# Softmax attention: 49-row stacks per head, two heads at a time in two 64-row tiles, four stack buffers, maxima in pairs

## Chip, core and metric

The kernel runs on one core of a Trainium2 chip. The metric is the device time of one execution in microseconds (us). Engines: PE is TensorE, PEld its weight loads, DVE VectorE, ACT ScalarE, POOL GpSimd, SP the engine that issues the DMAs. A name with q behind it (PEq) is that engine's sequencer.

## What is computed

The reference is a chain of two layers on x of shape (8, 1024, 256): softmax attention and routed experts, then linear attention and a gated mixture of experts. The change touches only the softmax attention:

```python
qkv = x @ w_attn
q, k, v = jnp.split(qkv, 3, axis=-1)          # 16 heads of 16 features, t = 1024
attn = jnp.einsum('bhqd,bhkd->bhqk', q, k) * scale
attn = jnp.where(causal[None, None], attn, -jnp.inf)
sm = jax.nn.softmax(attn, axis=-1)
out = jnp.einsum('bhqk,bhkd->bhqd', sm, v)
```

## The kernel before

`build` calls nine phases, one after the other, with all engines meeting between them. `phase_softmax_attention` (lines 288 to 643) works on 32 groups (8 batches times 4 groups of 4 heads, `GH`). For each head it stacks high and low halves of q and k along the partitions: q as high, high, low, low and k as high, low, high, low, 16 rows each, so that one product over the stack is the sum of the four part products. Row 64 (`SR`) of the q stack holds minus the row maximum and row 64 of the k stack holds ones; the rest up to 128 is zero. Three such buffers (`NBUF`) are filled in turn by 10 DMAs each (`load`, lines 403 to 410), the last of which puts zeros into the row of the maxima.

Each group goes through two score passes:

* The maxima pass, one group or more ahead. 39 pieces (`pieces`, `piece`, lines 545 to 559), each up to 512 columns wide in one of three PSUM buffers (`m_ps`, `MBUF`). A piece is one matmul for each of its heads and, where it lies on the diagonal, one bf16 matmul of an identity with a causal mask behind them. DVE reduces each piece to its maximum (line 493) and gives the buffer back (`m_free`). At the end the maxima are turned by PE (line 563), negated by ACT (line 505) and put into row 64 by a DMA (`row`, line 412).
* The score pass. 24 steps (`steps`): two halves h of the queries, key blocks k, and pairs p of heads. A step is two matmuls (line 578) into one of two buffers of `e_ps`, and one exponential on ACT (line 523) into `pr`. Two steps make a unit, 12 units a group. On the diagonal POOL masks the exponentials (line 475). Two units later (`LAG = 2`) `products` (line 582) multiplies them with v in four column tiles of 32, in plain float32, which the trace shows as 8 matmuls for each unit. The sums `o_ps` are copied by ACT (line 511) twice a group, and PE may start the next sums only when SP has seen that copy (`o_free`).

PE's order is written out by hand in `group` (line 598): step by step the wait for the exponential two steps back, the scores, the pieces that `share` gives to this step, and after each second step the products of an earlier unit. From step 19 (`MEND`) the pieces belong to the group after the next, and PE waits there for that group's stacks (`stack_loaded`, line 608). SP issues those loads in the same group, right after the first output (lines 423 to 426). PE executes in order: whatever stands behind a wait waits too.

## Time and profile before

| what | value |
|---|---|
| median of 3 runs | 4138.56 us (4131.36 to 4143.86) |
| span of the profiled execution | 4136.6 us, mean granted clock 0.892 |
| PE busy in the span | 3388.8 us (82%) |
| DVE, ACT, POOL busy in the span | 2384.2, 1507.4, 839.8 us |
| first and last score matmul of this phase | 303.9 and 1411.0 us |
| first and last matmul of the maxima pass | 265.4 and 1383.4 us |

The profiled execution has no other time than its span; the median of the runs is 2 us above it. Busy shares are averages over phases with different limits; the softmax attention is a little over a quarter of the span, and only its own rows say what bounds it. The start of a PE instruction is recorded and its end is modelled, so consecutive matmuls overlap in the rows by their latency.

### The profile page before, as it was taken

The numbers are of one execution on the slowest core, as the hardware profiler recorded it, in microseconds if no ns is written. First come the engines' busy times: TensorE is split into PE (matmuls) and PEld (weight loads), VectorE is DVE, ScalarE is ACT, GpSimd is POOL, SyncE is SP. The second block draws the span as 40 slices with busy tenths as digits, with TensorE's granted clock in tenths as the row PEclk, the third lists the DMA queues.
The fourth block names the chain that finished last, engine by engine and source line by source line (L and its number), as shares of the span: only waits on it lengthen the run. The fifth ranks groups of instructions, "written<-read, shape, count | busy, mean of one in ns | idle before, by whom it ended". The sixth has DMA issues, their size and how long they took to land. (4 is left out here: it accounts for less than half of the span.)

```text
span 4136.6 us, 62031 instructions
## 1 busy us (share of the span) xinstructions
PE 3388.8 (82%) x21377; PEld 2546.4 (62%) x21377; DVE 2384.2 (58%) x5007; ACT 1507.4 (36%) x2286; POOL 839.8 (20%) x1006
## 2 busy tenths in 40 slices
PE   6859999999999766579564776999566599999998
PEld 5735555555555465569343564777466488888887
DVE  5546666666666377683123785555477644444544
ACT  2315555555555433334002662000133323333333
POOL 0021111111111122234674663000122100000000
PEclk9879999999999878789656998999777699999999
DMA  6884666666666256563565996666344433233331
GB/s 191 234 146 60 85 85 85 85 81 84 84 85 84 74 184 200 183 214 127 132 139 138 345 346 217 210 207 206 108 153 153 158 84 85 86 81 81 81 81 51
DMA packets 452026, 570.37 MB, mean 138 GB/s; under 512 B 94544, under 2 KB 300400, under 8 KB 450672
## 3 DMA queue, kind: packets, MB, share of 16 engines
q1 hardware_dynamic: 440064, 544.45, 52.3%
q0 software_dynamic: 10240, 14.16, 2.0%
q10 hardware_dynamic: 1648, 10.81, 0.7%
q8 instruction: 42, 0.69, 0.1%
q14 instruction: 32, 0.26, 0.0%
HBM read 329.62 MB, written 238.61 MB: 137 GB/s over the span
## 5 line engine op out<-in xcount | busy, mean ns | idle before, releaser
L493 DVE TENSOR_REDUCE att_mx<-att_m_ps 128x1 f32<-128x512 f32 (+4 forms) x1248 | 743.5, 645 | 381.6 <-PE att_m_ps L554 324.1
L523 ACT ACTIVATE att_pr<-att_e_ps 128x1024 f32<-128x1024 f32 (+3 forms) x768 | 597.7, 811 | 366.5 <-PE att_e_ps L578 362.3
L551 PE MATMUL att_m_ps<-att_ks,att_qs 128*128 128x512 f32 (+3 forms) x1536 | 470.3, 377 | 99.5 <-PEq L39 95.4
L578 PE MATMUL att_e_ps<-att_qs,att_ks 128*128 128x512 f32 (+3 forms) x1536 | 466.9, 386 | 10.5 <-PEq L39 9.0
L475 POOL TENSOR_SCALAR_AFFINE_SELECT att_pr<-att_pr 128x256 f32<-128x256 f32 x512 | 206.7, 407 | 938.5 <-PEq L571 931.9
L578 PEld LDWEIGHTS att_e_ps<-att_qs,att_ks 128*128 128x128 f32 x1536 | 249.1, 194 | 239.9 <-issue 186.7
L551 PEld LDWEIGHTS att_m_ps<-att_ks,att_qs 128*128 128x128 f32 x1536 | 280.0, 195 | 155.2 <-issue 93.7
L594 PE MATMUL att_o_ps<-att_pr,att_vs 128*17 128x512 f32 (+3 forms) x3072 | 330.1, 502 | 0.0
L2116 DVE TENSOR_TENSOR ffn_hid<-ffn_gate,ffn_u_ps 128x512 f32<-128x512 f32 x192 | 132.1, 688 | 249.5 <-PE ffn_u_ps L698 213.1
L2164 ACT ACTIVATE ffn_hh<-ffn_hid 128x512 fp32r<-128x512 f32 x192 | 121.4, 633 | 421.5 <-DVE ffn_hid L2120 319.3
L698 PE MATMUL ffn_y_ps<-ffn_wld,ffn_hh 128*128 128x256 f32 x768 | 216.9, 282 | 0.0
L698 PE MATMUL ffn_y_ps<-ffn_whd,ffn_hh 128*128 128x256 f32 x768 | 216.2, 281 | 0.0
L2126 DVE TENSOR_TENSOR ffn_hl<-ffn_hid,ffn_hh 128x512 fp32r<-128x512 f32 x192 | 133.0, 693 | 141.7 <-ACT ffn_hh L2164 141.7
L698 PE MATMUL ffn_y_ps<-ffn_whd,ffn_hl 128*128 128x256 f32 x768 | 214.2, 279 | 0.0
L1059 PE MATMUL prj_t_ps<-prj_ident,prj_xn 128*128 128x128 f32 x256 | 62.7, 422 | 161.8 <-DVE prj_al L984 159.1
L554 PE MATMUL att_m_ps<-att_causal,att_identb 128*128 128x128 bf16 (+2 forms) x736 | 188.9, 257 | 0.0
L2086 POOL TENSOR_TENSOR ffn_rs<-ffn_ve,ffn_mhalf 128x4 f32<-128x4 f32 x16 | 16.1, 1007 | 824.7 <-POOLq L39 824.7
L698 PE MATMUL ffn_g_ps<-ffn_xh,ffn_whg 128*128 128x512 f32 x384 | 153.5, 400 | 28.0 <-DMA ffn_xl<-x_low 20.6
L1940 ACT ACTIVATE lin_ot<-lin_o_ps 128x1024 f32<-128x1024 f32 x32 | 32.9, 1027 | 367.1 <-PE lin_o_ps L1970 357.7
L2162 ACT ACTIVATE ffn_gate<-ffn_g_ps 128x512 f32<-128x512 f32 x192 | 114.5, 596 | 134.8 <-PE ffn_g_ps L698 134.8
L1059 PEld LDWEIGHTS prj_t_ps<-prj_ident,prj_xn 128*128 128x128 f32 x256 | 48.7, 219 | 172.3 <-DVE prj_al L984 168.0
L698 PE MATMUL ffn_g_ps<-ffn_xh,ffn_wlg 128*128 128x512 f32 x384 | 152.8, 398 | 0.0
(286 smaller groups left out, 8168.2 us busy)
## 6 DMA issues: line engine op xcount, KB each, us to landing
prj_o<-attended SPq DMA_DIRECT2D x32, 1024.0 KB, 5.0
ffn_wt<-weights SPq DMA_DIRECT2D x16, 2048.0 KB, 16.0
att_qs<-q_high SPq DMA_DIRECT2D x64, 256.0 KB, 5.8
att_qs<-q_low SPq DMA_DIRECT2D x64, 256.0 KB, 8.7
att_ks<-k_high SPq DMA_DIRECT2D x64, 256.0 KB, 12.3
att_ks<-k_low SPq DMA_DIRECT2D x64, 256.0 KB, 15.9
attended<-att_ot SPq DMA_DIRECT2D x64, 256.0 KB, 2.2
prj_x<-x SPq DMA_DIRECT2D x32, 512.0 KB, 5.9
```

Source lines behind the costliest of these rows:

```text
L475: e.affine_select(out=blk, in_=blk, compare_op=ALU.is_ge, fill=0.0, base=0, pattern=[[0, 2], [1, P]], channel_multiplier=-1).then_inc(mask ...
L493: e.reduce_max(mx[:, h, heads[0]:heads[-1] + 1, q], src, AX.X).then_inc(m_free, 1)
L523: e.activation(pr[:, u % NPR, 2 * p:2 * p + 2, 0:w], e_ps[:, s % 2, :, 0:w], ACT.Exp).then_inc(exp_done, 1)
L551: ins = e.matmul(out[:, i], qs[:, j, hd, q * P:(q + 1) * P], ks[:, j, hd, h * BLK:h * BLK + w], start=i == 0, stop=h != q // 4, skip_group ...
L554: ins = e.matmul(out[:, :, w - P:w], identb[:], causal[:].unsqueeze(1).broadcast_to((P, len(heads), P)), start=False, stop=True, skip_grou ...
L578: i = e.matmul(e_ps[:, s % 2, n, 0:w], ks[:, j, hd, k * P:(k + 1) * P], qs[:, j, hd, (h + 1) * BLK - w:(h + 1) * BLK], start=True, stop=True)
L594: i = e.matmul(o_ps[32 * hd:32 * hd + VW, BLK - w:BLK], vs[:, j, k, hd * VW:(hd + 1) * VW], pr[:, u % NPR, hd, 0:w], start=k == 0, stop=k ...
L698: i = e.matmul(out, a, b, start=first and n == 0, stop=last and n == len(terms) - 1, **kw)
L2116: product_ = e.tensor_tensor(hid[:, c % 2], gate[:, c % 2], u_ps[:, c % 2], ALU.mult)
L2126: e.tensor_tensor(hl[:, c % 3], hid[:, c % 2], hh[:, c % 3].bitcast(fp32), ALU.subtract).then_inc(hl_ready, 1)
L2162: e.activation(gate[:, c % 2], g_ps[:, c % 2], ACT.Silu).then_inc(gate_ready, 1)
L2164: e.activation(hh[:, c % 3], hid[:, c % 2], ACT.Copy).then_inc(hh_ready, 1)
```

## The change

The fourth part product (low times low) is dropped, so a stack has 48 rows and the row of the maxima is row 48. Two heads share one buffer: heads 0 and 1 of the group at partitions 0 to 48, heads 2 and 3 at 64 to 112. Each matmul of both passes then covers 48 or 49 rows from partition 0 or 64, and matmuls for the upper and the lower half follow each other in pairs, into different PSUM banks. The ones of the k stack are now written once, beside and beyond the stack's rows, so no DMA of zeros is needed, and the maxima product leaves their row out. There are four stack buffers, loaded by 12 smaller DMAs and one for v, three groups ahead. The row of the maxima is written by two DMAs.

The pieces come in pairs, one of each half: 21 pairs, 42 pieces. The masks of a diagonal pair come first (two bf16 matmuls over all 128 rows), then the score matmuls add to them. Units with at most 256 columns take one step with both head pairs, so there are 20 steps in 12 units. `products` stands at the head of a unit and takes the unit three back (`LAG = 3`), the same place in PE's order as before. The copy of the sums, though, is now made after the exponential of the third unit (`of_unit[LAG - 1]`) and of the seventh. PE turns to the group after the next at unit 8 (`TURN`) and takes the maxima at step 16 (`MAXIMA`), the first of unit 9.

```diff
-    NBUF = 3
+    NBUF = 4
     NPR = 4
     MBUF = 3
-    SR = 4 * HD
+    LAG = 3
+    HALF, MAXROW = P // 2, 3 * HD
-        qs = ph.sb("qs", [P, NBUF, GH, T], f32r)
-        ks = ph.sb("ks", [P, NBUF, GH, T], f32r)
+        qs = ph.sb("qs", [P, NBUF, 2, T], f32r)
+        ks = ph.sb("ks", [P, NBUF, 2, T], f32r)
...
-        steps = [(h, k, p) for h in range(2) for k in range(4 * h + 4) for p in range(2)]
+        units = [(h, k) for h in range(2) for k in range(4 * h + 4)]
+        steps = []
+        for u, (h, k) in enumerate(units):
+            steps += [(u, (0, 1))] if width(h, k) <= BLK // 2 else [(u, (0,)), (u, (1,))]
...
+                both = 2 * keys(q, h) <= BLK and q != 1
+                (partial if h == q // 4 else whole).extend((q, h, ps) for ps in (((0, 1),) if both else ((0,), (1,))))
+        pairs, taken = [], 0
+        for n, piece in enumerate(partial):
+            pairs.append(piece)
+            while taken < len(whole) and taken + 1 <= len(whole) * (n + 1) / len(partial):
+                pairs.append(whole[taken])
+                taken += 1
...
+        TURN, MAXIMA = 8, 16
...
                 def load(g, j):
-                    for name, dst, parts in (("qh", qs, (0, 1)), ("ql", qs, (2, 3)),
-                                             ("kh", ks, (0, 2)), ("kl", ks, (1, 3))):
-                        for r in parts:
-                            e.dma_start(dst[r * HD:(r + 1) * HD, j].bitcast(fp32), src_rows[name][g]
-                                        ).then_inc(stack_loaded[j], 16)
+                    for n in range(2):
+                        for dst, parts in ((qs, ("qh", "qh", "ql")), (ks, ("kh", "kl", "kh"))):
+                            for r, name in enumerate(parts):
+                                at = n * HALF + r * HD
+                                e.dma_start(dst[at:at + HD, j].bitcast(fp32), src_rows[name][g][:, 2 * n:2 * n + 2]
+                                            ).then_inc(stack_loaded[j], 16)
                     e.dma_start(vs[:, j], v_rows[g]).then_inc(stack_loaded[j], 16)
-                    e.dma_start(maxima_row(j), zero[:]).then_inc(stack_loaded[j], 16)
...
                     if loads:
-                        load(g + 2, (nxt + 1) % NBUF)
+                        load(g + 3, (nxt + 2) % NBUF)
...
-                        if s == 2 * LAG - 1 and not first:
+                        if s == of_unit[LAG - 1][0] and not first:
                             outputs(1, NPR)
-                        if s == 2 * (LAG + 3) + 1:
+                        if s == of_unit[LAG + 3][0]:
                             outputs(0, NPR + 4)
...
+                def maxima_pair(j, i):
+                    q, h, ps = pairs[i]
+                    w, masks = keys(q, h), h == q // 4
+                    out = [m_ps[:, (2 * i + n) % MBUF, 0:len(ps) * w].rearrange("p (n w) -> p n w", w=w)
+                           for n in range(2)]
+                    for n in range(2):
+                        if masks:
+                            e.wait_ge(m_free, 2 * i + n + 1)
+                            e.matmul(out[n][:, :, w - P:w], identb[:],
+                                     causal[:].unsqueeze(1).broadcast_to((P, len(ps), P)), start=True, stop=False,
+                                     skip_group_check=True)
+                    for m, p in enumerate(ps):
+                        for n in range(2):
+                            if not masks and m == 0:
+                                e.wait_ge(m_free, 2 * i + n + 1)
+                            rows = slice(n * HALF, n * HALF + MAXROW)
+                            ins = e.matmul(out[n][:, m], qs[rows, j, p, q * P:(q + 1) * P],
+                                           ks[rows, j, p, h * BLK:h * BLK + w], start=not masks and m == 0,
+                                           stop=m == len(ps) - 1, skip_group_check=True)
...
                 def scores(j, s):
+                    u, ps = steps[s]
+                    h, k = units[u]
                     w = width(h, k)
+                    for m, p in enumerate(ps):
+                        for n in range(2):
+                            rows = slice(n * HALF, n * HALF + MAXROW + 1)
+                            i = e.matmul(e_ps[:, s % 2, n, m * w:(m + 1) * w], ks[rows, j, p, k * P:(k + 1) * P],
+                                         qs[rows, j, p, (h + 1) * BLK - w:(h + 1) * BLK], start=m == 0,
+                                         stop=m == len(ps) - 1, skip_group_check=True)
...
+                    for u in range(UNITS):
+                        if not (first and u < LAG):
+                            products(j, u - LAG)
+                        if u == TURN and more2:
+                            e.wait_ge(stack_loaded[nxt2], LOADS)
+                            take(e, (stack_loaded[nxt2], LOADS))
+                        due = list(share[u]) if (more2 if u >= TURN else more) else []
+                        for s in of_unit[u]:
+                            for i in due[:1]:
+                                maxima_pair(nxt2 if u >= TURN else nxt, i)
+                            due = due[1:]
+                            exponentials(s, first)
+                            if s == MAXIMA and more:
+                                maxima()
+                            scores(j, s)
+                        for i in due:
+                            maxima_pair(nxt2 if u >= TURN else nxt, i)
```

## Rows read from the trace of the kernel before

**Rows 1.** Busy time in stretches of the stage, first and last of three: length, engines, clock.
```profile
core 0: us, PE busy (x) PEld busy (x) DVE busy (x) ACT busy (x) POOL busy (x), PEclk, DMA share, GB/s
304.00:650.00 346.00, 325.98 (x2093) 178.29 (x2093) 230.85 (x393) 194.34 (x264) 62.27 (x154) 0.98 0.58 77
...
1000.00:1411.00 411.00, 388.28 (x2544) 209.23 (x2545) 258.79 (x442) 237.42 (x327) 78.81 (x196) 0.99 0.54 75
```

**Rows 2.** Timeline of PE alone, two groups: start, length, instruction, idle before and its releaser.
```profile
827.39 0.63 PE L551 MATMUL att_m_ps<-att_ks,att_qs 128*128 128x128 f32 x4 [2.42 <-PEq L39]
...
862.50 0.64 PE L551 MATMUL att_m_ps<-att_ks,att_qs 128*128 128x128 f32 x4 [2.43 <-PEq L39]
```

**Rows 3.** Who waited for whom, 304 to 1411 us: total us, times, longest.
```profile
PE att_m_ps L551 <- PEq L39: 58.0, 29, 2.7
...
PEld att_e_ps L578 <- ACT att_pr L523: 43.9, 70, 0.9
...
PEld att_m_ps L551 <- DVE att_mx L493: 26.4, 68, 1.9
```

**Rows 4.** DMA issues, 304 to 1411 us: count, size, median us to landing.
```profile
att_qs<-att_zero SPq DMA_DIRECT2D x29, 16.0 KB, 17.0
```

**Rows 5.** Timeline of all engines, 803 to 822 us.
```profile
803.53 0.41 PE L594 MATMUL att_o_ps<-att_pr,att_vs 128*17 128x128 f32 x8
...
804.01 0.60 ACT L511 ACTIVATE att_ot<-att_o_ps 128x512 f32<-128x512 f32 x1
...
804.68 0.39 PE L551 MATMUL att_m_ps<-att_ks,att_qs 128*128 128x512 f32 x1
...
805.00 1.05 PE L594 MATMUL att_o_ps<-att_pr,att_vs 128*17 128x512 f32 x8
...
807.48 0.84 PE L594 MATMUL att_o_ps<-att_pr,att_vs 128*17 128x384 f32 x8
...
808.25 0.73 PE L578 MATMUL att_e_ps<-att_qs,att_ks 128*128 128x512 f32 x2
...
808.82 0.63 PE L551 MATMUL att_m_ps<-att_ks,att_qs 128*128 128x512 f32 x2
...
809.08 1.94 ACT L523 ACTIVATE att_pr<-att_e_ps 128x1024 f32<-128x1024 f32 x2 [1.39 <-PE att_e_ps L578]
...
809.29 0.62 PE L578 MATMUL att_e_ps<-att_qs,att_ks 128*128 128x512 f32 x2
...
809.92 3.28 SPq L410 DMA_DIRECT2D att_qs<-att_zero  x1
...
822.31 1.05 PE L594 MATMUL att_o_ps<-att_pr,att_vs 128*17 128x512 f32 x8
```

**Rows 6.** Timeline of the weight loads (PEld): one alone, two together, then eight of products.
```profile
276.18 0.19 PEld L551 LDWEIGHTS att_m_ps<-att_ks,att_qs 128*128 128x128 f32 x1 [0.41 <-DVE att_mx L493]
...
277.97 0.30 PEld L551 LDWEIGHTS att_m_ps<-att_ks,att_qs 128*128 128x128 f32 x2 [0.41 <-DVE att_mx L493]
...
819.30 0.13 PEld L594 LDWEIGHTS att_o_ps<-att_pr,att_vs 128*17 128x17 f32 x8 [0.31 <-issue]
```

**Rows 7.** Groups by line and shape, 304 to 1411 us: busy, mean ns, idle before.
```profile
L493 DVE TENSOR_REDUCE att_mx<-att_m_ps 128x1 f32<-128x512 f32 x744 | 475.3, 685 | 103.3 <-PE att_m_ps L551 54.4 <-PE att_m_ps L554 47.9
L523 ACT ACTIVATE att_pr<-att_e_ps 128x1024 f32<-128x1024 f32 x384 | 379.3, 1027 | 225.0 <-PE att_e_ps L578 224.4
```

**Rows 8.** Timeline of the start: the first group's reduces, a DMA issue, the first scores.
```profile
269.29 20.10 DVE L493 TENSOR_REDUCE att_mx<-att_m_ps 128x1 f32<-128x384 f32 x35 [0.25 <-PE att_m_ps L554]
...
278.97 11.89 SPq L410 DMA_DIRECT2D att_qs<-att_zero  x1
...
303.93 1.19 PE L578 MATMUL att_e_ps<-att_qs,att_ks 128*128 128x512 f32 x2 [9.00 <-PEq L39]
```

**Rows 9.** Busy time in two stretches of the start, columns as in rows 1.
```profile
275.00:280.00 5.00, 4.55 (x17) 2.48 (x17) 5.00 (x9) 0.00 (x0) 0.00 (x0) 1.00 1.03 121
...
283.00:287.00 4.00, 4.00 (x12) 2.20 (x11) 4.00 (x9) 0.00 (x0) 0.00 (x0) 0.57 1.19 170
```

More of the change, by code:

```diff
@@ L363, in keys @@
             return min(BLK, (q + 1) * P - h * BLK)
+        units = [(h, k) for h in range(2) for k in range(4 * h + 4)]
+        UNITS = len(units)
+        steps = []
+        for u, (h, k) in enumerate(units):
+            steps += [(u, (0, 1))] if width(h, k) <= BLK // 2 else [(u, (0,)), (u, (1,))]
+        NS = len(steps)
+        of_unit = [[s for s in range(NS) if steps[s][0] == u] for u in range(UNITS)]
         def diagonal(s):
-            h, k, p = steps[s]
+            h, k = units[steps[s][0]]
@@ L367, in diagonal, with masks_before @@
             return k * P >= h * BLK
+        NDIAG = sum(diagonal(s) for s in range(NS))
+        def masks_before(u):
+            return sum(diagonal(s) for v in range(-LAG, u + 1) for s in of_unit[v % UNITS])
+        whole, partial = [], []
+        for q in range(KB):
+            for h in range(q // 4 + 1):
+                both = 2 * keys(q, h) <= BLK and q != 1
+                (partial if h == q // 4 else whole).extend((q, h, ps) for ps in (((0, 1),) if both else ((0,), (1,))))
+        pairs, taken = [], 0
@@ L369, in shares @@
+        for n, piece in enumerate(partial):
[3 more added lines that the diff above has]
+                taken += 1
+        NPAIR, NPC = len(pairs), 2 * len(pairs)
+        TURN, MAXIMA = 8, 16
+        assert NPC % MBUF == 0 and taken == len(whole) and width(*units[steps[MAXIMA][0]]) <= BLK - P
+        assert MAXIMA % 2 == 0 and steps[MAXIMA][0] > TURN
         def shares():
-            order = list(range(MEND, len(steps))) + list(range(MEND))
@@ L372, in shares @@
-            load = [keys(q, h) * len(heads) + 96 for q, h, heads in pieces]
-            work = [width(*steps[s][:2]) + 160 for s in order]
+            order = list(range(TURN, UNITS)) + list(range(TURN))
+            load = [keys(q, h) * len(ps) + 64 for q, h, ps in pairs]
+            work = [sum(width(*units[u]) * 2 * len(steps[s][1]) + 80 for s in of_unit[u]) for u in order]
             out, n, done, due = {}, 0, 0.0, 0.0
-            for s, w in zip(order, work):
+            for u, w in zip(order, work):
@@ L376, in shares @@
                 due += w * sum(load) / sum(work)
-                out[s] = []
-                while n < NPC and done + load[n] / 2 <= due:
+                out[u] = []
+                while n < NPAIR and done + load[n] / 2 <= due:
                     done += load[n]
-                    out[s].append(n)
+                    out[u].append(n)
                     n += 1
+            assert n == NPAIR
             return out
         share = shares()
-        NDIAG = sum(diagonal(s) for s in range(len(steps)))
@@ L386, in phase_softmax_attention @@
-        UNITS = len(steps) // 2
-        LAG = 2
-        def masks_before(u):
-            return sum(diagonal(2 * (v % UNITS)) for v in range(-LAG, u + 1)) * 2
         src_rows = {n: d.rearrange("(g h d) t -> g d h t", h=GH, d=HD)
```

154 lines of the change are left out of this document (58 added, 96 removed).

## The prediction

> **What bounds the stage now.** I read the slices of the span for where this phase lies, then busy time in stretches, the timeline of one group, the waits, the issues of SP, and the groups by shape. PE is busy 94% of the stage, DVE 63 to 67%, ACT 56 to 58%, at a granted clock of 0.98 or 0.99, so the 2.4 GHz level nearly throughout [rows 1]. The same piece comes again 862.50 - 827.39 = 35.1 us later [rows 2]: that is one group, and 31 such periods make up the stage. PE bounds it, but its busy time hides drains and its own order. Inside each period it stands still once, 2.42 us, at the sequencer's wait for the stacks of the group after the next [rows 2]; in all 58.0 us in 29 waits [rows 3]. SP issued the last DMA of that load at 809.92 and such a DMA lands 17.0 us later [rows 4, 5], hence at 827, which is when PE goes on.
>
> **One group before, in PE's time.** A score pass has 4608 columns for each head (the unit widths 512, 384, 256, 128, four times 512, and again 512 to 128), 18432 for four. At 2.4 GHz 512 columns take 0.213 us, a pass 7.7, two passes 15.4. Eight product matmuls take 1.05 us for 512 columns and 0.41 for 128 [rows 5], that is four times the clock for each column, with the four heads side by side: 4608 columns give 7.7 us. Masks: 32 blocks of 128 columns, 1.7. A weight load of 128 columns costs 0.11 where it isn't hidden, two of them taking 0.30 and one 0.19 [rows 6]; so a 128-column block costs 0.11 instead of 0.053, which adds 1.7 for scores, pieces and masks. Going over to the products and back: two scores behind products take 0.73 instead of 0.62 and start 0.07 before the products' modelled end (808.25 against 807.48 + 0.84), where they otherwise start 0.16 to 0.17 before it (809.29 against 808.82 + 0.63) [rows 5]: 0.21 on the way out. Products start 0.07 before the end of the piece ahead (805.00 against 804.68 + 0.39) [rows 5]: 0.10 on the way in. 12 units, 3.7. Turning the maxima 0.3. Sum 30.5. Waits: 2.4 for the stack, and 43.9 and 26.4 us over 31 periods for exponentials and reduces [rows 3], 2.3. Total 35.2 against 35.1.
>
> **What the change takes away.**
> * The stack wait. Loads are issued a whole period earlier, and there is no DMA of zeros behind them: -2.4 a group. Issuing costs SP 13 DMAs instead of 10, some 0.4 us each more, hidden because the next output isn't ready for several units. The two rows of the maxima are issued at unit 9, units 10 and 11 hide their landing.
> * The streams. If two row tiles run at the same time, both passes go from 15.4 to 7.7 us. No row of this trace shows two row tiles. Bounds: nothing gained (0), all (7.7). The nearest row are the four column tiles of the products, which share the array fully, and whose eight weight loads take 0.13 us together [rows 5, 6]. I take the whole 7.7, with the loads of a pair side by side too.
>
> **What it adds.**
> * Mask excursions. Masks cover 128 rows, the matmuls around them 64, so 13 of the 21 pairs now leave the row tiles and come back. Price from both sides: 0, if full and half height mix freely, or that of the products' excursion with a load of 128 columns exposed on the way in, 0.10 + 0.11 = 0.21 and 0.21 back. Seven of the 13 stand directly behind products, where one of the two is paid anyway: 7 x 0.21 + 6 x 0.42 = 4.0 us. Narrow pairs cost their load (0.4 a pass, 8 blocks of 128 as 4 pairs: 4 x 0.054 = 0.2 each, 0.4 together), and 26 masks at 0.11 cost 2.8 instead of 1.7. The sum of work is then 7.7 + 7.7 + 2.8 + 0.4 + 3.7 + 4.0 + 0.3 = 26.6, or 22.6 without excursions.
> * Waits on DVE. A reduce of 512 columns takes 0.685 [rows 7] and follows the last by 0.6 (35 in 20.1 us, [rows 8]). A pair needs two of three buffers, so its second matmul waits for the first reduce of the pair before: latency 0.2 (1.05 less 4 x 0.213), hand-over 0.1 (808.25 + 0.73 to ACT's start at 809.08) [rows 5], reduce 0.6, hand-over 0.1, 1 us after that pair's stream ended, while the scores between give 0.21 only. I walked PE through the 12 units with these numbers: products, switch, masks, pair, scores, pair, scores. A unit of 512 with one masked and one whole pair, at its head the products of 512: 0.95 products, 1.16 masks begin, 1.5 to 1.7 pair, 1.92 scores, second tile of the next pair only at 2.6 to 2.8, scores to 3.0. Before, such a unit took the same 3.0 (819.30 to 822.31) [rows 5, 6]. The waits come to 0.5 in unit 0, 0.4 in 2, 1.3 in 4, 0.6 in 5, 0.8 in 6, 0.7 in 7, 0.7 in 8: 5.0.
> * The copy of the sums. Before, the copy started at 804.01, behind the exponential of the second unit, ended at 804.61, and the products that need it started at 805.00 with nothing to spare [rows 5]. Now it stands behind an exponential of 1.03 us [rows 7] of the third unit, whose scores come after the previous products. PE reaches the products of the new sums while that exponential and the 0.60 copy run. I find 1.1 us of stall in unit 2 and 0.5 in unit 6. Queued behind it are the scores of the next unit, and behind them ACT.
>
> The walk gives 26.6 + 5.0 + 1.6 = 33.2 us a group; without mask excursions part of the time is waited for DVE anyway, and it gives 30.3. The truth should lie nearer the row-derived price: I take 32.0. DVE needs 36 times 0.6 us for 18432 columns and a start for six pieces more, about 23 us, and ACT was busy 0.57 x 35.1 = 20: neither binds, though both are nearer.
>
> One rule speaks against the change here. The Trainium skill, TensorEngine Tiling (Array Packing), Key Properties, says that changing the tiling mode, not just the tile, drains TensorE. By that rule the 0.21 each way stands and the period is 33.2; the trace agrees for the products (0.73 against 0.62). No row shows it for masks.
>
> **The start.** Three loads before took from 243.8 to 303.9, when the row of the first maxima landed behind them (SP waits 11.89 us to issue the last, PE 9.00 [rows 8]). Now four smaller loads, 7.4 MB instead of 7.2, stand in front of that row: 0 to 2 us later. I take 2.
>
> **Sum.** 31 periods x (35.1 - 32.0) = 96 us less, 2 more: span 4136.6 - 94 = 4042.6, and the median stands 2.0 above the span: 4045 us.
>
> **Rivals.**
> 1. Cheap excursions: full and half height mix with hardly a drain, DVE's waits stay. Period 28 to 31, say 30.3: 4138.6 - 149 + 2 = 3992, down to 3920. For it: masks and scores mixed before without a drain, and of the products' 0.21 out only the exposed load is a plain cost. 20%.
> 2. Row tiles overlap in part: a pair of 512 takes 0.28, a third of the way from 0.213 to twice that. Then 7.7 / 3 = 2.5 a group comes on top, period 34.5, 4122 us. 13%. The Trainium skill, TensorE: Matmul & The Clock Gate, Measured speedup vs the span model, has four row tiles gain 3.07 instead of 4, which by that figure is about this case; no run here shows it.
> 3. Row tiles do not overlap: 7.7 back on the 33.2 of the walk, of which some 4 fall into the waits for DVE: period 36.9, +56 and 2: 4197 us, slower. It decides from a pair of 512 that takes over 0.3 us. Against it: the column tiles. 9%.
> 4. The waits eat all of it: the copies and the hand-overs of pairs cost 3 us more than walked, period 34.7 to 35.5, about 4138. 8%.
> 5. The clock falls. In the start PE, held up by DVE, kept 1.00 in one stretch (275 to 280) and fell to 0.57 in another (283 to 287) [rows 9]. If a fifth of each period ran at 1.2 GHz, 26.6 / 5 = 5.3 us more, period 37, about 4200. Against it: 18.6 of the 32 us are streamed, 58%, and the stretch that kept its clock streamed 0.21 of each 0.6 us. 8%.
>
> **Chances.** The forecast itself (period 31 to 34, 4014 to 4106) 42%. Within 0.3%, 12 us, a measurement can't tell it from no change. Faster: forecast, rival 1 and nearly all of rival 2, 0.74; same 0.08 (rivals 2 and 4); slower 0.18 (rivals 3, 5, a rest of 4). The range of 3940 to 4160 leaves out the lower part of rival 1 and rivals 3 and 5.
>
> **What would show it.** The wait of PEq before the pieces is gone (if not, the loads are late: first step wrong). The starts of the two matmuls of a pair lie within a few ns and the next pair follows after 0.21 (streams). The masks' weight loads start only at the end of the stream before and the loads behind them again (excursions). PE waits on DVE in front of the second matmul of pairs, and an idle of about 1 us stands in front of the products of each group's fourth unit, released by SP (copy). If DVE's reduces follow each other at 0.6 throughout, DVE has become the bound and the period is nearer 25; if PEclk falls under 0.9, rival 5 it is.

## The result, and the profile after

The changed kernel takes 4274.25 us (median of 4 runs, 4258.38 to 4283.74) against 4140.42 for the kernel before on the same chip: ratio 1.0324, 95% interval 1.0296 to 1.0352. It is slower, by 134 us, and lies above the range of 3940 to 4160. The profiled execution has a span of 4256.7 us and a mean granted clock of 0.828 (before 0.892).

The page of the profile after, the slices of the span: 40 slices of 106 us, the stage lies in the third to the fifteenth.

```profile
PE   6869999999999966649765575999766679999998
...
PEclk9967886687777878869956798999877689999999
```

PE is as full as ever, but the clock it was granted stands at 6 to 8 tenths of full speed through the stage. Busy time in stretches of the changed kernel, columns as in [rows 1]; the last three rows are neighbours inside one group.

```profile
320.00:650.00 330.00, 300.80 (x1898) 118.52 (x1895) 203.31 (x372) 168.80 (x199) 51.63 (x107) 0.79 0.37 60
650.00:1000.00 350.00, 323.78 (x1848) 124.55 (x1846) 200.44 (x363) 167.04 (x194) 47.41 (x98) 0.70 0.40 61
...
1400.50:1435.20 34.70, 31.65 (x222) 12.66 (x221) 23.64 (x44) 19.51 (x24) 5.83 (x12) 0.90 0.43 70
1422.00:1424.00 2.00, 1.24 (x7) 0.46 (x11) 1.98 (x4) 2.00 (x3) 0.00 (x0) 0.95 1.08 137
1424.00:1430.00 6.00, 6.00 (x27) 1.66 (x20) 2.68 (x5) 2.28 (x3) 0.00 (x0) 0.50 0.88 133
1430.00:1432.00 2.00, 1.93 (x18) 1.07 (x15) 0.76 (x2) 0.62 (x1) 0.00 (x0) 0.84 0.00 0
```

[Rows 1] had 0.98 and 0.99 here. A period, taken from one negation of the maxima by ACT (L513) to the next, is 39.3 us in the mean: 327.83 to 1506.87 for 30 of them. Five of them are 34.7 at a clock of 0.90, one is 33.7 at 0.95, and the longest are 48.0 at 0.56. A clock of 0.56 in the mean is the 1.2 GHz level nearly throughout.

What stood in [rows 2] is gone: no 2.4 us in front of the maxima pass. The timeline of the changed kernel's PE shows what has come in its place (L574 maxima pass, L601 scores, L566 masks, L618 products):

```profile
804.18 1.48 PE L618 MATMUL att_o_ps<-att_pr,att_vs 128*17 128x384 f32 x8 [3.24 <-PEq L39]
...
1405.38 0.51 PE L574 MATMUL att_m_ps<-att_ks,att_qs 48*128 48x512 f32 x2
1405.72 0.40 PE L601 MATMUL att_e_ps<-att_qs,att_ks 49*128 49x512 f32 x2
1406.05 0.23 PE L566 MATMUL att_m_ps<-att_causal,att_identb 128*128 128x128 bf16 x1
1406.67 0.23 PE L566 MATMUL att_m_ps<-att_causal,att_identb 128*128 128x128 bf16 x1 [0.38 <-DVE att_mx L501]
...
1408.05 0.29 PE L566 MATMUL att_m_ps<-att_causal,att_identb 128*128 128x128 bf16 x2
1408.27 0.50 PE L574 MATMUL att_m_ps<-att_ks,att_qs 48*128 48x512 f32 x2
...
1412.25 1.05 PE L618 MATMUL att_o_ps<-att_pr,att_vs 128*17 128x512 f32 x8 [0.82 <-issue]
...
1421.53 0.40 PE L574 MATMUL att_m_ps<-att_ks,att_qs 48*128 48x512 f32 x1
1422.24 0.50 PE L574 MATMUL att_m_ps<-att_ks,att_qs 48*128 48x512 f32 x1 [0.31 <-DVE att_mx L501]
...
1423.49 1.65 PE L618 MATMUL att_o_ps<-att_pr,att_vs 128*17 128x512 f32 x8 [0.52 <-PEq L39]
...
1428.12 1.91 PE L618 MATMUL att_o_ps<-att_pr,att_vs 128*17 128x512 f32 x8
```

Four things are to be read there. A pair of row tiles takes 0.40 us (1405.72) and one tile alone 0.40 as well (1421.53): they run at the same time (two full-height ones took 0.62, [rows 5]). The copy of the sums holds PE up twice a group, by 0.82 and 0.52. Behind the second of these the same products that took 1.05 take 1.65 and then 1.91: the clock has dropped, as the window from 1424 to 1430 shows. And once in every four groups PE stands still for some 3 us in the middle of a unit, 3.24 at 804.18. That one was in no step of the forecast. The DMA queues of the page point to what it is:

```profile
q8 instruction: 96, 1.57, 0.2%
```

Before, there were 42 such transfers. The kernels of this study with three groups in the loop's body had 41 to 44 and lack the stall. Those with four had 96 or more and have it, but for one (5, below), whose program is shorter: it had 41 and lacks the stall. So the length of the body decides and not the number of groups: with the stall it holds 876 matmuls of PE or more (4 x 219 in the first kernel of 8, 4 x 221 here), without it at most 780 (4 x 195 in that of 5). The loop body became four groups long (`NBUF = 4`) instead of three, and PE seems to wait for its own instructions each time the loop turns; that it waits for these transfers is inferred from their number, no row ties a transfer to a stall. The Trainium skill, Runtime: NRT & Kernel Launch, Instruction fetch mechanics, says that a taken branch whose target is outside the two pages held has to fetch it by DMA first. By that rule such a stall is what a longer body brings; the trace agrees, 2.6 to 3.4 us at each of the loop's returns.

### The profile page after: what moved, and what is told of

It is laid out like the page before. It is cut to its first block and busy times, and to the rows that moved or that the text cites. A ratio compares the mean times of both kernels' runs of the same rounds, so it can differ in the third digit from the quotient of the medians.

```text
span 4256.7 us, 62197 instructions
## 1 busy us (share of the span) xinstructions
PE 3480.3 (82%) x21473; PEld 2414.6 (57%) x21473; DVE 2386.0 (56%) x5103; ACT 1507.8 (35%) x2158; POOL 802.5 (19%) x872
## 5 line engine op out<-in xcount | busy, mean ns | idle before, releaser
L536 ACT ACTIVATE att_pr<-att_e_ps 128x1024 f32<-128x1024 f32 (+2 forms) x640 | 593.8, 938 | 539.0 <-PE att_e_ps L601 536.3
L574 PE MATMUL att_m_ps<-att_ks,att_qs 48*128 48x512 f32 (+3 forms) x1536 | 457.1, 520 | 18.0 <-DVE att_mx L501 16.2
L618 PE MATMUL att_o_ps<-att_pr,att_vs 128*17 128x512 f32 (+3 forms) x3072 | 423.7, 630 | 55.2 <-PEq L39 30.3
L484 POOL TENSOR_SCALAR_AFFINE_SELECT att_pr<-att_pr 128x256 f32<-128x256 f32 (+1 forms) x384 | 186.4, 486 | 1103.3 <-PEq L592 1067.8
L601 PE MATMUL att_e_ps<-att_qs,att_ks 49*128 49x512 f32 (+3 forms) x1536 | 346.2, 439 | 2.8 <-ACT att_pr L536 2.6
L574 PEld LDWEIGHTS att_m_ps<-att_ks,att_qs 48*128 48x128 f32 x1536 | 206.3, 229 | 240.3 <-DVE att_mx L501 127.0
L566 PEld LDWEIGHTS att_m_ps<-att_causal,att_identb 128*128 128x128 bf16 x832 | 64.4, 101 | 366.1 <-DVE att_mx L501 211.0
L566 PE MATMUL att_m_ps<-att_causal,att_identb 128*128 128x128 bf16 (+1 forms) x832 | 179.8, 274 | 62.4 <-PEq L39 29.8
L601 PEld LDWEIGHTS att_e_ps<-att_qs,att_ks 49*128 49x128 f32 x1536 | 190.0, 235 | 69.5 <-issue 57.5
L1966 ACT ACTIVATE lin_ot<-lin_o_ps 128x1024 f32<-128x1024 f32 x32 | 32.9, 1029 | 367.2 <-PE lin_o_ps L1996 357.9
```

Of the source, the lines that this page charges most:

```text
L484: e.affine_select(out=blk, in_=blk, compare_op=ALU.is_ge, fill=0.0, base=0, pattern=lead + [[1, P]], channel_multiplier=-1).then_inc(maske ...
L536: e.activation(out, src, ACT.Exp).then_inc(exp_done, 1)
L566: e.matmul(out[n][:, :, w - P:w], identb[:], causal[:].unsqueeze(1).broadcast_to((P, len(ps), P)), start=True, stop=False, skip_group_chec ...
L574: ins = e.matmul(out[n][:, m], qs[rows, j, p, q * P:(q + 1) * P], ks[rows, j, p, h * BLK:h * BLK + w], start=not masks and m == 0, stop=m ...
L601: i = e.matmul(e_ps[:, s % 2, n, m * w:(m + 1) * w], ks[rows, j, p, k * P:(k + 1) * P], qs[rows, j, p, (h + 1) * BLK - w:(h + 1) * BLK], s ...
L618: i = e.matmul(o_ps[32 * hd:32 * hd + VW, BLK - w:BLK], vs[:, j, k, hd * VW:(hd + 1) * VW], pr[:, u % NPR, hd // 2, hd % 2, 0:w], start=k ...
```

## The experiments

The theory after the comparison: everything that was sized came out about as sized, and what decided is rival 5, PE falling to the 1.2 GHz level behind its stalls. Rival theories: row tiles overlap worse than they look, or mask excursions (leaving the row tiles for a mask of 128 rows and coming back) and waits cost more than priced, with the clock a mere companion. Eighteen kernels were run. Where one leaves out part of the computation this is said; the others do all of it or add to it. Ratios are to the kernel before on the same chip; differences in us are between medians, partly of different chips, on which the kernel before took 4140 to 4150 us.

**1. The copies of the sums.** The outputs are taken ahead of the exponential again:

```diff
+                        if s == of_unit[LAG - 1][0] and not first:
+                            outputs(1, NPR)
+                        if s == of_unit[LAG + 3][0]:
+                            outputs(0, NPR + 4)
                         if s == of_unit[u][0]:
                             e.wait_ge(pv_done, u + 1)
...
                         e.activation(out, src, ACT.Exp).then_inc(exp_done, 1)
-                        if s == of_unit[LAG - 1][0] and not first:
-                            outputs(1, NPR)
-                        if s == of_unit[LAG + 3][0]:
-                            outputs(0, NPR + 4)
```

> The changed kernel with the copies of the sums moved ahead of the exponential of units 2 and 6, so that PE's products of the new sums no longer stand 0.9 and 1.5 us behind them. Theory 1 (the row tiles themselves lower the granted clock, because PE streams less): only the two stalls go, some 1.6 us a group or 50 us, the clock of the stage stays below 0.85, about 4210 us. Theory 2 (the new stalls are what makes the clock fall, and it would stay up without them): the clock comes back above 0.93 and the time goes to 4030 to 4080 us.

4141.6 us, ratio 0.9989 (0.9958 to 1.0020): 133 us less than the changed kernel, and between what the two theories of the expectation gave. Busy time of this kernel in two periods and behind the loop's return:

```profile
740.07:783.90 43.83, 40.18 (x221) 15.45 (x219) 23.67 (x44) 19.61 (x24) 5.80 (x12) 0.65 0.32 56
814.79:845.69 30.90, 28.58 (x221) 11.92 (x220) 23.57 (x44) 19.46 (x23) 5.80 (x12) 1.00 0.52 79
...
744.00:746.00 2.00, 0.20 (x6) 0.05 (x2) 1.02 (x2) 0.60 (x1) 0.00 (x0) 1.00 0.03 8
746.00:748.00 2.00, 0.83 (x10) 0.22 (x10) 0.00 (x0) 0.00 (x0) 0.64 (x1) 1.00 0.03 8
748.00:750.00 2.00, 1.62 (x10) 0.94 (x10) 1.29 (x2) 1.02 (x1) 0.64 (x1) 0.67 0.00 0
750.00:760.00 10.00, 9.97 (x60) 3.65 (x56) 4.62 (x8) 4.64 (x6) 2.26 (x5) 0.50 0.36 82
760.00:770.00 10.00, 9.86 (x52) 4.41 (x49) 5.85 (x11) 4.58 (x5) 0.64 (x1) 0.50 0.96 132
```

About half of the groups now take 30.9 us, at a clock of 1.00. In the group behind each loop's return PE stands still for 3 us (2.98 in front of 747.17), the clock falls to 0.50, and with PE busy 19.83 of the 20 us from 750 on it stays there: the period is 43.8. A stall of 3 us costs 13. The DMA queues carry next to nothing while the clock falls (share 0.03 and 0.00 from 744 to 750), so it is not the loads that lower it.

**2. The same order in full height.** The stacks of before (128 rows, one head each) in the changed order, with its pairs, buffers and copies:

```diff
-                            rows = slice(n * HALF, n * HALF + MAXROW)
-                            ins = e.matmul(out[n][:, m], qs[rows, j, p, q * P:(q + 1) * P],
...
+                            ins = e.matmul(out[n][:, m], qs[:, j, 2 * n + p, q * P:(q + 1) * P],
```

> The changed kernel's order, pairs, buffers and copies, but with the stacks of before: 64 rows and the maxima, padded to 128, every matmul over the full height, so both passes stream 15.4 us a group instead of 7.7. Theory 1: the clock of the stage comes back above 0.93 and the kernel is faster than the changed one in spite of 7.7 us more of streaming, 4100 to 4200 us. Theory 2: the stalls are still there, so the clock dips stay too, and the streams come on top: 4350 us or more.

4162.0 us, ratio 1.0057 (1.0040 to 1.0074). The same with the copies moved as in 1:

> The changed kernel's order with full-height stacks (4162 us) and with the copies of the sums ahead of the exponentials of units 2 and 6. In row tiles this move gained 133 us. If that gain was the stall alone, it is 1.6 us a group and the same here: about 50 us, 4112. If the stall in row tiles cost most by the clock behind it, the gain here, where the clock is 1.00, is 30 to 60 us and two thirds of the 133 were the clock. If it gains over 100 us here too, the clock had nothing to do with it.

4112.9 us, ratio 0.9919 (0.9897 to 0.9940). Stretches of the first:

```profile
650.00:1000.00 350.00, 326.73 (x2207) 178.87 (x2206) 238.27 (x434) 197.04 (x232) 59.07 (x122) 1.00 0.62 85
```

Twice the streamed columns, and the kernel is 112 us faster than the changed one, although its larger loads delay the first scores to 333.5 us (297.1 in the changed kernel). Periods are 34.3 and 32.5 us, the ones at the loop's return 36.6 to 38.0 and 34.8 to 36.4. The stall is 2.1 to 2.6 us here and costs 2.3 to 3.9: itself and at most a short dip of the clock (0.95 in one period of 36.0). The copies cost 49 us in full height, where the clock stays, against 133 in row tiles. If the stalls alone are worth the same in both, 84 of the 133 were the clock; that split is an estimate.

**3. Three buffers, and both.** Row tiles with loads two groups ahead and a loop body of three groups (`NBUF = 3`), with late copies and with early ones:

> The changed kernel with three stack buffers, loaded two groups ahead, so the loop body holds three groups and not four. Theory 1 and 2: if the 3.3 us stall of PE in front of a group's first products, once in four groups, belongs to the length of the loop body, it goes: seven times 3.3 us and the clock lost behind it, 4220 to 4250 us. If it has another cause, or if the wait for the stacks comes back (2.4 us a group before), no gain or 4300 us.

> The changed kernel with both mends: copies of the sums ahead of the exponentials, and three stack buffers, so three groups in the loop body. If the two gains of 133 and 59 us add up, 4080 us; the loop-return stall goes (7 times 3.3 us) and the clock is at 0.87 to 0.9. If both gains were the same clock time, 4120 to 4140 us.

4215.0 us, ratio 1.0166 (1.0138 to 1.0193), clock 0.78 from 650 to 1000; and 4133.0, ratio 0.9984 (0.9961 to 1.0007). The loop's stall is gone in both. But the gains of 59 and 133 us do not add. In the second the most frequent period is now 34.1 us (13 of 31 are 34.0 or 34.1), at a clock of 0.85; a few are 30.9 at 1.00. In one of them, 543.06 to 577.14, PE's rows show no stall of over 0.4 us; the clock leaves 1.00 between 555 and 560, where two waits for DVE of 0.31 and 0.30 stand, is at 0.50 from 560 to 570, and is back at 1.00 behind that. Loads are in flight there too (DMA share 1.0 from 555 to 570), as they are in the periods that keep their clock, so this view alone doesn't say which of the two made it fall. Why this kernel falls more often than that of 1, which has the longer stalls, stays open.

**4. Twice the streams, in row tiles.** Every matmul of both passes is issued twice, still in pairs, so that 15.4 us a group are streamed again. Where a pair has masks, the first copy stands ahead of them:

> The changed kernel with the matmuls of both passes issued twice into the same place, the second time as before, so the row tiles stream 15.4 us a group, as much as the full-height version a_full does, and PE has 7.7 us more to do. Theory A (what keeps the clock up is how much PE streams, row tiles counting like any): the clock of the stage is above 0.93 and the time 4160 to 4230 us, faster than the changed kernel with half the work. Theory B (matmuls in row tiles keep the clock up less than full-height ones, however many there are): the clock stays below 0.85 and the time rises above 4400 us.

4403.5 us, ratio 1.0584 (1.0532 to 1.0637), clock 0.98, 0.85 and 0.87 in the three long stretches. Undisturbed periods are 40.3, those at the loop's return up to 60.9.

```profile
357.37:397.70 40.33, 38.96 (x317) 19.98 (x315) 24.07 (x43) 19.74 (x24) 5.79 (x13) 1.00 0.34 60
```

Neither theory of the expectation holds whole: between stalls the clock is 1.00 with row tiles too, but behind a stall it falls, which full height of the same streamed time (2) hardly does.

**5. No masks in the maxima pass.** Both kernels take their maxima over the masked keys too. In the changed kernel, and in the kernel of 7:

> The changed kernel without the causal masks in the maxima pass (the maximum then runs over all keys of a block, an upper bound for the softmax). 26 full-height bf16 matmuls and 13 leaves from the row tiles go: at one clock 2.8 + 4.0 us a group, a part of it already hidden behind waits for DVE, so 60 to 150 us off at an unchanged clock of about 0.76 in the stage, 4120 to 4210 us. If full-height matmuls are what kept the clock from falling further, the clock falls and less or nothing is gained.

> The kernel before's order with three part products in full-height stacks (the kernel of 4057 us), without the causal masks in the maxima pass, so its maxima are over masked keys too. Masks there cost 32 loads and streams of 128 columns, 1.7 x 2 = about 3 us a group with their loads, and no change of tile height. If the masks of the changed kernel cost excursions on top, this one gains less than the 88 us that leaving them out gained there, some 50 to 90 us at full clock, 3970 to 4010; if masks cost what their columns and loads cost in either kernel, both gain the same after the clock is taken out.

4186.0 us, ratio 1.0089 (1.0070 to 1.0108), 88 less than with masks although the clock falls to 0.69; and 4005.0, ratio 0.9663 (0.9643 to 0.9683), 52 less. Masks and excursions cost time in row tiles, but with fewer full-height matmuls the stage of row tiles has a lower clock; the full-height kernel stays at 1.00 without its masks. The first kernel also lacks the loop's stall (41 instruction transfers, its program is shorter), which blurs its 88.

**6. Added work.** A full-height bf16 matmul of 512 columns ahead of each mask in the changed kernel, as it stands with late copies and four buffers:

```diff
+                            e.matmul(m_ps[:, (2 * i + n) % MBUF].rearrange("p (n w) -> p n w", w=P), identb[:],
+                                     causal[:].unsqueeze(1).broadcast_to((P, 4, P)), start=True, stop=True,
+                                     skip_group_check=True)
                             e.matmul(out[n][:, :, w - P:w], identb[:],
```

> The changed kernel with one more full-height bf16 matmul of 512 columns ahead of each mask (26 a group, 26 x 0.213 = 5.5 us a group at 2.4 GHz, 172 us over 31 groups). If full-height work is what holds the clock up, the stage's clock rises from 0.76 over 0.9 and most of the extra work is paid by the clock: 4170 to 4290 us. If the clock falls because PE waits too much or because of the tiles whatever stands beside them, it stays near 0.8 and the extra work is paid in full: 4370 to 4450 us.

4214.4 us, ratio 1.0164 (1.0142 to 1.0185). It does 172 us more work than the changed kernel (31 x 26 x 0.213) and is 60 us faster.

```profile
650.00:1000.00 350.00, 322.57 (x2293) 127.72 (x2291) 219.53 (x400) 184.50 (x216) 55.73 (x115) 0.98 0.42 65
...
740.00:776.30 36.30, 33.91 (x248) 13.42 (x246) 23.54 (x44) 19.68 (x23) 5.80 (x12) 1.00 0.40 63
```

Does any streamed column help, or full-height ones? Two kernels with float32r matmuls of 512 columns in one place, ahead of a masked pair, once as pairs of row tiles and once in full height:

> The changed kernel with two pairs of row-tile matmuls of 512 columns ahead of the masks of each masked pair: 26 x 0.213 = 5.5 us a group more streamed at 2.4 GHz, in row tiles instead of full height. If any streamed column counts, the stage's clock is 0.97 as with the full-height ones and the time 4200 to 4240 us. If work in row tiles counts for little, the clock stays at 0.76 to 0.9 and the time lies at 4290 to 4400.

> Control of the run with added row-tile pairs: the same place, the same waits and the same streamed time, as two full-height float32r matmuls of 512 columns. Clock 0.95 or more and 4200 to 4240 us if the added full-height work holds the clock, as the bf16 ones did.

4645.5 us, ratio 1.1211 (1.1172 to 1.1250), against 4363.6, ratio 1.0542 (1.0515 to 1.0569). Both are over what was expected, probably because the added matmuls wait for both buffers first, which the bf16 ones did not. But the kernel with the pairs is 282 us slower than the one in full height. Little of that is the way in and out of the row tiles, which the pairs add where they stand directly behind products: periods with a clock of 1.00 take 40.3 us in the one and 39.2 in the other, 1.1 us or some 34 us in all. The rest is the clock; several periods of the first kernel take 51.2 at about 0.70. The same stretch of the one and of the other:

```profile
650.00:1000.00 350.00, 327.53 (x1854) 128.68 (x1847) 162.05 (x295) 135.18 (x157) 39.68 (x82) 0.73 0.31 48
```

```profile
650.00:1000.00 350.00, 316.78 (x2026) 135.44 (x2018) 193.93 (x353) 161.85 (x189) 49.23 (x102) 0.91 0.34 56
```

**7. The clock by itself.** Stretches of 40 rounds ahead of the changed kernel's maxima pass. In each round PE issues k matmuls (or k pairs) of 512 columns and waits for one DVE reduce:

```diff
+                        for r in range(k):
+                            for n in ((0, 1) if kind == "rows" else (r % 2,)):
+                                ins = e.matmul(m_ps[:, n], ks[rows, 0, n, 0:P], ks[rows, 0, n, 0:BLK], start=True,
+                                               stop=True)
+                        ins.then_inc(go, 1)
```

> The changed kernel with twelve stretches put ahead of its maxima pass. In each, 40 times, PE runs k pairs of 512-column float32r matmuls and then waits for one DVE reduce of about 0.6 us. k is 2, 4, 8, 12, and each k is run in three forms: in pairs of row tiles (2k matmuls of 49 rows, about k x 0.21 us if they overlap), full height (k matmuls of 128 rows, the same streamed time), and one row tile alone (k matmuls of 49 rows). Theory A, that only the share of time in which columns are streamed sets the clock: the three forms of one k have the same granted clock, and it rises with k. Theory B, that matmuls of 49 rows count for less than those of 128: at some k, where both stream the same time, the full-height stretch stands at 1.00 and the row tiles at 0.5 to 0.8, and one tile alone at or below the pair. The stretches alone add some 40 x 12 x 2.2 = 1000 us.

> The same stretches ahead of the changed kernel's maxima pass with other numbers of matmuls between two hand-overs, in this order: 6 full height, 6 row-tile pairs, 7 pairs, 7 full height, 7 of 98 rows in full height, 7 pairs, 7 full height, 8 of 98 rows, 8 pairs, 5 full height, 5 pairs, 9 in one tile alone. The first probe had pairs and full height alike at 4 (clock 0.50) and at 8 (0.98 and 1.00). If pairs count like full height, the clocks of the two forms are the same at 5, 6 and 7 too. If pairs count less, there is a number of matmuls at which full height stands at 1.00 and pairs below 0.9, and then 98 rows in full height tell whether it is the rows used (98 rows fall as well) or the tiles (98 rows stay up).

Each kernel was run once (5847.6 and 5920.0 us with the stretches), so every stretch is one measurement of 40 rounds. The first, with k = 8: pairs, full height, one tile alone.

```profile
861.85:980.10 118.25, 84.11 (x624) 64.99 (x624) 26.98 (x39) 0.00 (x0) 0.00 (x0) 0.98 0.00 0
983.04:1097.48 114.44, 80.30 (x312) 55.52 (x312) 26.99 (x39) 0.00 (x0) 0.00 (x0) 1.00 0.00 0
1100.41:1280.12 179.71, 145.60 (x312) 95.70 (x312) 26.95 (x39) 0.00 (x0) 0.00 (x0) 0.50 0.00 0
```

The second, in its order: 6 in full height, 6 pairs, 7 pairs, 7 in full height, 7 of 98 rows.

```profile
261.66:360.37 98.71, 64.58 (x234) 41.64 (x234) 26.95 (x39) 0.00 (x0) 0.00 (x0) 0.98 0.37 49
362.90:508.58 145.68, 111.62 (x468) 75.33 (x468) 26.92 (x40) 0.00 (x0) 0.00 (x0) 0.52 0.00 0
512.80:677.76 164.96, 130.84 (x546) 91.04 (x546) 26.95 (x39) 0.00 (x0) 0.00 (x0) 0.50 0.00 0
681.96:787.73 105.77, 71.61 (x273) 48.21 (x273) 26.97 (x39) 0.00 (x0) 0.00 (x0) 1.00 0.00 0
790.44:948.28 157.84, 123.74 (x273) 80.22 (x273) 26.92 (x39) 0.00 (x0) 0.00 (x0) 0.54 0.00 0
```

At k = 4 and fewer all forms stood at 0.50, at 8 pairs and full height at 0.98 or more. Between them, at 6 and 7, the forms part: full height is granted the 2.4 GHz level and pairs of the same streamed time the 1.2 GHz level. Later stretches of the same run repeat this at 7: 0.50 for pairs, 0.98 for full height. At 5 pairs stood at 0.50, and full height, behind a stretch at 1.00, at 0.66. A third form, one full-height matmul of 98 rows, which is what a pair uses, falls too when it follows full height at k = 7 (0.54), and stands at 1.00 at 8, as pairs do: here it is the rows in use, not the tiles. It is not what the rows hold: in the kernel before rows 65 to 127 of the stacks are zero, and its clock is 0.98 or more. Nor is it the loads: no data moved in these stretches (DMA share 0.00 in all but the first of each run). One tile alone stayed at 0.50 even with 12 matmuls, 0.86 of the time busy (212.66 of 246.81 us).

**8. What the change did not need.** The kernel before with four buffers and loads three groups ahead and nothing else:

> The kernel before with four stack buffers, loaded three groups ahead, and nothing else. Both theories: the wait for the stacks of 2.4 us a group goes and with it the dips of the clock behind it, 4055 to 4075 us, period 32.5 us. If the wait is only replaced by another, no change.

4101.4 us, ratio 0.9911 (0.9894 to 0.9927), less of a gain than expected. Periods are 32.4 to 32.5 us, 2.6 less than [rows 2]; it gives part of that back at the loop's return (36.1 every fourth period) and at the start, where the row of the maxima queues behind three full loads (first scores at 319.8 us instead of 303.9). And the kernel before with three buffers and three part products, in full height, which makes the loads 7 DMAs instead of 10 and needs no row of zeros:

```diff
-    SR = 4 * HD
+    SR = 96
...
-                    for name, dst, parts in (("qh", qs, (0, 1)), ("ql", qs, (2, 3)),
-                                             ("kh", ks, (0, 2)), ("kl", ks, (1, 3))):
+                    for name, dst, parts in (("qh", qs, (0, 1)), ("ql", qs, (2,)),
+                                             ("kh", ks, (0, 2)), ("kl", ks, (1,))):
...
-                    e.dma_start(maxima_row(j), zero[:]).then_inc(stack_loaded[j], 16)
```

> The kernel before, full height and its own order, three buffers, with one part of the change: the fourth part product is dropped, so a group's stacks take 6 DMAs and 1.6 MB instead of 8 and 2.1, and the maxima stand in row 96 with no DMA of zeros (the maxima pass leaves that row out). The load should land some 4 us earlier, ahead of PE's wait for it: no wait, period 32.5 us, and the start some 13 us shorter because fewer bytes stand ahead of the first row of maxima: 4040 to 4060 us. If the wait is not set by the bytes but by when SP issues, 4110 us or more.

4057.3 us, ratio 0.9782 (0.9766 to 0.9798), the best of all kernels with the whole computation. Its clock is 1.00 in all three long stretches, its periods are 32.6 us, and it has neither the stack wait nor the loop's stall.

**9. A little added work.** In the changed kernel with early copies, full-height matmuls of 128 columns ahead of each mask, with four buffers; with three; and of 256 columns with three:

> The changed kernel with the copies of the sums moved (4141 us, clock 0.86) and one more full-height bf16 matmul of 128 columns ahead of each mask, 26 x 0.11 = 2.9 us a group with its load, or 90 us. At full clock throughout this order would take 4214 - 172 - 49 = 3993 us without and some 4080 with the extra work. If so little full-height work lifts the clock, 4060 to 4120, below 4141 though it does more; if it lifts nothing, 4200 to 4240.

> The changed kernel with early copies, three buffers (so no stall at the loop's return) and a full-height bf16 matmul of 128 columns ahead of each mask. With four buffers the periods at full clock took 31.8 us with this extra work and 30.9 without; the loop's return made every fourth 40 to 43, and others took 35 to 36 at a lower clock. If the clock now holds, the periods are 31.8 throughout: 4141 - 31 x (35.1 - 31.8) = 4039 us, under the 4057 of the full-height kernel with three part products. If the waits for DVE still let it fall in most periods, as in the same kernel without extra work (4133), 4090 to 4135.

> The same with 256 columns of full-height work ahead of each mask, 26 x 0.053 = 1.4 us a group more. If the first holds the clock already, this one is 1.4 x 31 = 43 us slower at 4080. If the first does not and this one does, periods of about 33.2 us and 4080; if neither does, 4110 to 4170.

4141.0 us, ratio 1.0005 (0.9994 to 1.0017); 4109.9, ratio 0.9910 (0.9882 to 0.9937); 4096.0, ratio 0.9872 (0.9856 to 0.9889). The first does 90 us more work than the kernel of 1 in the same time, which lies between what was expected with and without a lift of the clock. The other two do more work than the 4133.0 of 3 and are 23 and 37 us faster, by the ratios 31 and 46. Where the clock holds, their periods are 31.9 and 32.9; with 256 columns it holds nearly everywhere. Row tiles can be held up in this way, but not below the 4057 of full height with three part products.

## Why the prediction was wrong, step by step

**The step that failed is the one that left the clock alone: the loss by a falling clock was put at nothing in the sum.** The sum took the 2.4 GHz level for the whole period, as in [rows 1], and the fall was rival 5 at 8%, 4200 us. It came true, and larger: 39.3 us a period against the 37 given there. Two arguments were set against it, both wrong in kind. The first counted streamed time (58% of the period) as if a streamed column were a column whatever its height; in the stretches of 7, 98 rows in use hold the clock up less than 128 at the same streamed time. The second took one stretch of [rows 9] that kept its clock between short waits; it was full-height work. And the stalls that the forecast itself had found, 1.1 and 0.5 us for the copies, were priced at their own length. In the group shown above the first, 0.82 at 1412.25, costs no more than that, but the second, 0.52 at 1423.49, is followed by some 6 us at 1.2 GHz. So it is over the stage: of the stalls that found the clock at 1.00, the longer first one was followed by a fall in 3 of 24 groups, the shorter second one in 9 of 13. The length of a stall alone doesn't decide.

**At full clock the forecast comes out, as an estimate.** No run has the changed kernel at a clock of 1.00; its nearest period is 33.7 us at 0.95. The order without the copies' stalls takes 30.9 us at 1.00. With the 0.82 and 0.52 of those stalls that makes 32.2, with the 1.8 that the copies cost a period in full height 32.7, where 32.0 was forecast. From the other side, the kernel of 6 has periods of 36.3 at 1.00, and without the added 5.5 at least 30.8, since part of the added work may fall into waits. That 4214 less 172 is 4042 and 4045 was forecast is in part luck: that kernel also pays six returns of the loop, some 5 us each, which no forecast had. And the 32.0 was itself chosen between two sums, 30.3 and 33.2. The remaining 7.1 us of the 39.3 are, over 31 periods, 220 us; less the 9 by which the start came out shorter than forecast that is 211, and the profiled execution took 213 more than the 4045. Of the 220 the loop's stalls themselves are 6 times about 3, some 18 us. The rest, about 200, is put down to the low clock by difference.

* *Stack wait, -2.4.* Right: gone, and 2.6 a period where it alone was removed (8).
* *Streams, -7.7.* The overlap is full, 0.40 for two as for one, so rivals 2 and 3 are out. The Trainium skill's figure (TensorE: Matmul & The Clock Gate, Measured speedup vs the span model), 3.07 for four tiles, has no counterpart here: two tiles of 512 gave 2. What it bought was less. In the same order with early copies, full height takes 32.5 a period and row tiles 30.9: 1.6 us of the 7.7 arrive. The rest goes into excursions, exposed loads and waits for DVE (PE is idle 2.3 us of the 30.9 and 0.2 of the 32.5); no run separates them. Had the overlap been lost, rival 3's 36.9 would rather have been too low: the kernel of 4, which streams the full 15.4 in row tiles, takes 40.3 at a clock of 1.00.
* *Excursions, 0.21 each way.* From masks back to row tiles right: masks start at 1408.05, the pair behind them 0.22 later, of which 0.11 is their own streams, and its second tile another 0.10 later (0.50 against 0.40). From row tiles to masks it is less: masks start 0.33 after a pair (1405.72, 1406.05), which is 0.12 over its stream of 0.21, not 0.21. By these rows the sum of 4.0 was somewhat high. Whole periods leave room for more: at equal streamed time, order and clock (1.00), the kernel of 4 takes 40.3 and the full-height one 34.3. The 6.0 between them hold the excursions and the exposed loads, for which the forecast had 4.4, and with them those that the doubling itself adds. The Trainium skill, TensorEngine Tiling (Array Packing), Key Properties, has a change of mode drain TensorE; the trace agrees in kind.
* *Waits for DVE, 5.0.* In a period of 30.9 PE is idle for 2.3 us in all, but modelled ends hide part of the waits, so their own sum isn't settled by rows. DVE is busy 23.6 us of each period, where about 23 was forecast; it never became the bound.
* *Copies, 1.1 and 0.5.* Right in place and about in size, 0.82 and 0.52; wrong in what they bring with them.
* *Start, +2.* Wrong by 9 us, to the good: first scores at 297.1 us instead of 303.9, since the row of the first maxima was issued at 288.15 and not held up behind the loads.
* *The loop's return.* Missed, a second term put at nothing. Lengthening the body from three groups to four was taken as free, and it costs 2.6 to 3.4 us six times, besides the low clock behind them.

What stays open is how far each single wait for DVE of 0.3 to 0.4 us is to blame for a fall. That they suffice is seen in periods of 34.1 us without a longer stall, and that periods of 30.9 exist in the same kernel with such waits too. Taking them away altogether, with a fourth buffer for the maxima, wasn't tried. That rows in use matter is shown; by what measure they count is not.

## What to carry to other kernels

A change that makes PE stream less can lose on the clock what it wins in columns: before packing two small matmuls into row tiles, look at how many rows of the array are in use between the full-height work, and at every stall of PE, because behind any of them the same work may take up to twice as long. When PE's clock is lower after a change, price the change at full clock first (added full-height work that makes a kernel faster is a quick proof), and then remove the stalls. Here 2.6 us a group came from loads that came in time (35.1 to 32.5) and 1.6 at most from row tiles (32.5 to 30.9, both with early copies); three part products gave the first in full height, with seven DMAs a group and the old order.

## What was not expected of the hardware

* Added work made a kernel faster: 172 us of full-height matmuls, 4274 to 4214 us.
* A stall of 3 us cost 13 in row tiles (30.9 to 43.8), one of 2.1 to 2.6 us 2.3 to 3.9 in full height (34.3 to 36.7 at the least disturbed): with PE 99% busy behind it in row tiles, the clock stayed at the 1.2 GHz level for over 20 us.
* One row tile of 49 rows alone never left the 1.2 GHz level in its stretches, with PE busy up to 86% of the time.
* A loop body of four groups instead of three brought 96 instruction transfers instead of 42, and 2.6 to 3.4 us of standstill of PE at each return. With the masks left out the body of four had 41 transfers and no standstill.
